# A Strassen-Winograd product schedule on one Trainium2 core: one block product moved two places forward, degree products spread between matmuls

## What is computed

```python
h   = xn @ gnn_W                                  # 1250x1024 by 1024x1024
deg = 1 + number of edges into a node;  dinv = deg ** -0.5
gnn = relu(segment_sum(h[src] * dinv[src] * dinv[dst], dst) + b)      # with self loops
mix = linear attention: relu(xn Wq + bq) (relu(xn Wk + bk)^T (xn Wv + bv)) Wo + bo
x   = x + gnn + mix
x   = x + ffn(layernorm(x))                       # 8-bit fake quantised gate, up and down
```

## Time and profile before

| what | us |
|---|---|
| median of three runs | 723.74 (723.11 to 725.48) |
| the profiled execution, time | 723.66 |
| its span in the trace | 721.9 |
| TensorE busy in the span | 703.2 |
| VectorE, GpSimd, ScalarE busy | 548.6, 347.2, 234.4 |
| block products of h (420 matmuls), first to last start | 362.2 to 457.1 |
| the ten degree products (20 passes) | 367.78 to 369.9 |

### The profile page before, as it was taken

How to read it: one execution, slowest core, us unless ns; L and a number is a source line. 1 busy time by engine, 2 the same in 40 slices (tenths; PEclk the granted TensorE clock), 3 DMA queues, 4 the chain that set the end, 5 groups by cost and what they waited for, 6 DMA issues and landing times.

```text
span 721.9 us, 11607 instructions
## 1 busy us (share of the span) xinstructions
PE 703.2 (97%) x3800; PEld 362.3 (50%) x3800; DVE 548.6 (76%) x1035; ACT 234.4 (32%) x384; POOL 347.2 (48%) x441
## 2 busy tenths in 40 slices
PE   5998999999999999999999999999999999999996
PEld 3454555545555554566654444444444444445752
DVE  7878887887666778876697865869977778766766
ACT  5133334553333356554223334530100000003641
POOL 3676767888666778874254540011111111113317
PEclk9999999999999999999999999999999999999999
DMA  9825413563000000000000005153322132100707
GB/s 347 253 59 118 109 36 83 169 238 120 0 0 0 1 2 1 1 0 1 1 1 0 1 1 177 56 175 67 100 73 57 50 84 65 35 12 1 118 1 284
DMA packets 52804, 52.27 MB, mean 72 GB/s; under 512 B 36515, under 2 KB 37547, under 8 KB 52753
## 3 DMA queue, kind: packets, MB, share of 16 engines
q1 hardware_dynamic: 52752, 51.61, 24.4%
HBM read 37.96 MB, written 5.12 MB: 60 GB/s over the span
## 4 chain that ended last, share of the span: by engine, by line
PE 77%; DVE 8%; issue 5%; POOL 3%; DMA 3%; SPq 2%; ACT 1%; DVEq 1%; POOLq 0%
PE bank L632 17%; PE bank L872 13%; PE bank L745 12%; PE bank L709 12%; PE bank L816 12%; PE bank L920 3%; PE bank L614 2%; DVE mem L1491 2%; PE bank L949 2%; DVE counts L1368 1%; PE bank L652 1%; PE bank L808 1%; DMA mem<-in_x 1%; POOL hot_src L490 1%; ACT mem L977 1%
## 5 line engine op out<-in xcount | busy, mean ns | idle before, releaser
L632 PE MATMUL bank<-mem 128*128 128x512 f16 x960 | 222.7, 381 | 0.0
L490 POOL TENSOR_SCALAR hot_src<-iota_p,src_col 125x128 bf16<-125x128 bf16 x252 | 189.6, 767 | 14.1 <-issue 14.1
L632 PEld LDWEIGHTS bank<-mem 128*128 128x128 f16 (+1 forms) x960 | 91.0, 98 | 95.6 <-issue 1.6
L1368 DVE TENSOR_TENSOR counts<-bank,counts 128x120 f32 x328 | 92.1, 281 | 43.3 <-PE bank L614 6.3
L872 PE MATMUL bank<-mem 128*128 128x512 f16 (+1 forms) x504 | 105.5, 369 | 0.0
L709 PE MATMUL bank<-mem 128*128 128x512 f16 (+2 forms) x576 | 105.1, 339 | 0.0
L745 PE MATMUL bank<-mem 128*128 128x512 f16 x420 | 92.8, 384 | 0.0
L816 PE MATMUL bank<-mem 128*128 128x512 f16 x400 | 88.0, 379 | 0.3 <-DVE mem L1674 0.3
L872 PEld LDWEIGHTS bank<-mem 128*128 128x128 f16 x504 | 49.3, 98 | 53.7 <-issue 0.3
L709 PEld LDWEIGHTS bank<-mem 128*128 128x128 f16 (+1 forms) x576 | 55.3, 98 | 41.3
L573 POOL TENSOR_TENSOR cols<-cols 128x1 f32<-128x1 f32 x10 | 5.5, 555 | 138.9 <-DVE cols L1701 138.9
(11 more groups left out here) (179 smaller groups left out, 828.9 us busy)
## 6 DMA issues: line engine op xcount, KB each, us to landing
mem<-in_x SPq DMA_DIRECT2D x18, 512.0 KB, 4.0
out_x<-mem SPq DMA_DIRECT2D x9, 512.0 KB
mem<-in_L_mix_Wk SPq DMA_DIRECT2D x4, 1024.0 KB, 9.6
mem<-in_L_mix_Wv SPq DMA_DIRECT2D x4, 1024.0 KB, 8.4
mem<-in_L_mix_Wq SPq DMA_DIRECT2D x4, 1024.0 KB, 5.1
mem<-in_L_gnn_W SPq DMA_DIRECT2D x4, 1024.0 KB, 7.5
mem<-in_L_mix_Wo SPq DMA_DIRECT2D x4, 1024.0 KB, 6.2
mem<-in_L_ffn_w_down SPq DMA_DIRECT2D x4, 352.0 KB, 3.2
```

The source lines that it names most:

```text
L490: pool.tensor_scalar(hot_src[0:EC, i, c, :], iota_p[0:EC, :], src_col[0:EC, i, c:c + 1], None, ALU.is_equal).then_inc(S["hot_src_ready"], 1)
L632: last = pe.matmul(o[:, :], xT[:, a * K + k, bass.ds(t * P, P)], w16[i][:, k, b, :], start=(at == 0), stop=(at == len(parts) - 1))
L1368: dve.tensor_tensor(window, agg[i][:, k * WC:(k + 1) * WC], window, ALU.add).then_inc(S["adj_added"], 1)
```

## The change

In all five pairs B21 becomes the third product: B11, T4, B21, T2, T1, T3, B22. The waits that count products in g_full are renumbered (T2 is now the fourth, T1 the fifth). b0 is thus finished in mid-pair, and for j > 0 its rounding (h_high and h_low of block 0) moves forward on ScalarE and VectorE. On ScalarE keep_p5(j) now comes behind s_high(j+1, 2). keep_p1(0) moves ahead of s_high(0, 4). In pair 0 the degree product of tile n is issued ahead of matmul n of T2, for the first ten of T2's twelve matmuls, and no longer as a block of its own ahead of T2.

```diff
@@ -383,7 +383,7 @@
             load_wo(0, 1)
             sp.wait_ge(S["g_full"], 7 * (PAIRS_OF_TILES - 1) + 1)
             load_wo(1, 0)
-            sp.wait_ge(S["g_full"], 7 * (PAIRS_OF_TILES - 1) + 4)
+            sp.wait_ge(S["g_full"], 7 * (PAIRS_OF_TILES - 1) + 5)
             load_wo(1, 1)
             sp.wait_ge(SM["prod_full"], PAIRS)
             sp.dma_start(gb_b, gnn_b.rearrange("(a n) -> a n", a=1).broadcast_to([P, D])).then_inc(SM["gb_in"], 16)
@@ -736,10 +736,19 @@
                                   stop=True).then_inc(SE["e_mm"], 1)
             q_blocks(2, 1)
 
-            def product(j, left, right, o, fresh):
+            def degree(n):
+                return pe.matmul(agg[0][:, n:n + 1], sources[:, n * P:(n + 1) * P], ones, start=True, stop=True,
+                                 skip_group_check=True)
+
+            def product(j, left, right, o, fresh, degrees=0):
 
                 for k in range(K // 2):
-                    for a, b in ((0, 0), (0, 1), (1, 0)):
+                    for pass_n, (a, b) in enumerate(((0, 0), (0, 1), (1, 0))):
+                        n = 3 * k + pass_n
+                        if n < degrees:
+                            counted = degree(n)
+                            if n == degrees - 1:
+                                counted.then_inc(SM["deg_full"], 1)
                         block = s_half[j % 2][:, 2 * (left - 1) + a, k, :] if isinstance(left, int) else \
                             block_at(left[1], 2 * j + left[0], a)[:, k, :]
                         last = pe.matmul(o[:, :], block, g_w[right][:, k, b, :], start=(fresh and k == 0 and a == b),
@@ -761,14 +770,10 @@
                     pe.wait_ge(S["h_lo"], 4 * (j - 2) + 2)
                 product(j, (1, 1), "T4", b2, True)
 
+                pe.wait_ge(SG["p1_kept"], j + 1)
+                product(j, (0, 1), "B21", b0, False)
                 if j == 0:
                     pe.wait_ge(SM["sources"], 1)
-                    for n in range(T):
-                        last = pe.matmul(agg[0][:, n:n + 1], sources[:, n * P:(n + 1) * P], ones, start=True, stop=True,
-                                         skip_group_check=True)
-                    last.then_inc(SM["deg_full"], 1)
-
-                if j == 0:
                     pe.wait_ge(S["q_lo"], 3 * K + 1)
                 elif j == 1:
                     pe.wait_ge(SM["deg_ready"], 1)
@@ -776,7 +781,7 @@
                 else:
                     pe.wait_ge(SG["u3"], j - 1)
                 pe.wait_ge(SG["s_lo"], 4 * j + 2)
-                product(j, 2, "T2", b1, True)
+                product(j, 2, "T2", b1, True, T if j == 0 else 0)
 
                 if j == 0:
                     pe.wait_ge(SM["max_col"], 1)
@@ -786,8 +791,6 @@
                     pe.wait_ge(S["h_lo"], 4 * (j - 2) + 4)
                 product(j, 1, "T1", b3, True)
 
-                pe.wait_ge(SG["p1_kept"], j + 1)
-                product(j, (0, 1), "B21", b0, False)
                 pe.wait_ge(SG["s_lo"], 4 * j + 4)
                 pe.wait_ge(SG["u2"], j + 1)
                 product(j, 3, "T3", b1, False)
@@ -1072,8 +1075,16 @@
                     act.wait_ge(S["g_full"], 7 * (j - 1))
                 act.activation(s_half[j % 2][:, 2 * (i - 1)], s_sum[i - 1], ACT.Copy).then_inc(SG["s_hi"], 1)
 
-            for i in range(1, 5):
+            def keep_p1(j):
+                act.wait_ge(S["g_full"], 7 * j + 1)
+                if j > 0:
+                    act.wait_ge(SG["u3"], j)
+                act.activation(g_s1, g_bank[j % 2][0][:, :], ACT.Copy).then_inc(SG["p1_kept"], 1)
+
+            for i in range(1, 4):
                 s_high(0, i)
+            keep_p1(0)
+            s_high(0, 4)
             act.wait_ge(SC["clip_in"], 32)
             act.activation(clip[:, 2:4], clip[:, 0:2], ACT.Exp, scale=-1.0).then_inc(SC["exp"], 1)
 
@@ -1083,14 +1094,14 @@
                                o.rearrange("p (k n) -> p k n", n=P), ACT.Copy, scale=dinv_up[:, t:t + 1]).then_inc(S["h_hi"], 1)
 
             def keep_p5(j):
-                act.wait_ge(S["g_full"], 7 * j + 4)
+                act.wait_ge(S["g_full"], 7 * j + 5)
                 if j > 0:
                     act.wait_ge(SG["c22"], j)
                 act.activation(g_s5, g_bank[j % 2][3][:, :], ACT.Copy).then_inc(SG["p5_kept"], 1)
 
             def wo_high(n, c):
                 act.wait_ge(SM[f"wo_in{n}_{c}"], 16)
-                act.wait_ge(S["g_full"], 7 * (PAIRS_OF_TILES - 1) + (7 if n else 3))
+                act.wait_ge(S["g_full"], 7 * (PAIRS_OF_TILES - 1) + (7 if n else 4))
                 act.activation(wo16[n][:, c * (K // 2):(c + 1) * (K // 2), 0, :], wo[n][c], ACT.Copy,
                                scale=W_UP).then_inc(SM["wo_hi"], 1)
 
@@ -1103,22 +1114,25 @@
             for j in range(PAIRS_OF_TILES):
                 last_pair = j == PAIRS_OF_TILES - 1
                 b0, b1, b2, b3 = g_bank[j % 2]
-                act.wait_ge(S["g_full"], 7 * j + 1)
                 if j > 0:
-                    act.wait_ge(SG["u3"], j)
-                act.activation(g_s1, b0[:, :], ACT.Copy).then_inc(SG["p1_kept"], 1)
+                    keep_p1(j)
                 if j + 1 < PAIRS_OF_TILES:
                     s_high(j + 1, 1)
+                if j > 0:
+                    act.wait_ge(S["g_full"], 7 * j + 3)
+                    h_high(2 * j, 0, b0[:, :])
+                if j + 1 < PAIRS_OF_TILES:
+                    s_high(j + 1, 2)
                     keep_p5(j)
-                    for i in range(2, 5):
-                        s_high(j + 1, i)
+                    s_high(j + 1, 3)
+                    s_high(j + 1, 4)
                 else:
                     wo_high(0, 0)
                     keep_p5(j)
                     wo_high(0, 1)
-                act.wait_ge(S["g_full"], 7 * j + 5)
-                act.wait_ge(SM["dinv"], 3)
-                h_high(2 * j, 0, b0[:, :])
+                if j == 0:
+                    act.wait_ge(SM["dinv"], 3)
+                    h_high(0, 0, b0[:, :])
                 act.wait_ge(SG["c21"], j + 1)
                 h_high(2 * j + 1, 0, b2[:, :])
                 act.wait_ge(SG["c22"], j + 1)
@@ -1511,7 +1525,7 @@
             dve.tensor_reduce(flags[:, 1:2], agg[1][0:1, 0:P], AX.X, ALU.max).then_inc(SM["max_col"], 1)
 
             def u2(j):
-                dve.wait_ge(S["g_full"], 7 * j + 3)
+                dve.wait_ge(S["g_full"], 7 * j + 4)
                 dve.wait_ge(SG["p1_kept"], j + 1)
                 if j > 0:
                     dve.wait_ge(SG["c12"], j)
@@ -1571,11 +1585,13 @@
             for j in range(PAIRS_OF_TILES):
                 b0, b1, b2, b3 = g_bank[j % 2]
                 more = j + 1 < PAIRS_OF_TILES
-                if j > 0:
-                    u2(j)
                 if more:
                     s_low(j + 1, 1)
                     s2(j + 1)
+                if j > 0:
+                    h_low(j, 1, 2 * j, 0, b0[:, :])
+                    u2(j)
+                if more:
                     s_low(j + 1, 2)
                     s_low(j + 1, 3)
                     s4(j + 1)
@@ -1585,7 +1601,8 @@
                     wo_low(0, 1)
                     dve.wait_ge(SM["wo_lo"], 2)
                     a_tile(0, 0)
-                h_low(j, 1, 2 * j, 0, b0[:, :])
+                if j == 0:
+                    h_low(0, 1, 0, 0, b0[:, :])
                 dve.wait_ge(S["g_full"], 7 * j + 6)
                 if j > 0:
                     dve.wait_ge(SG["c21"], j)
```

## The result

The changed kernel takes 729.12 us (median of four runs, 728.52 to 729.82), the kernel before 723.88 us: the ratio is 1.0074, 95% interval 1.0059 to 1.0089. The profiled execution took 728.52 us with a span of 726.7, against 723.66 and 721.9: 4.86 us more.

A forecast was written before the change was run, and what follows sets the result against it. TensorE, busy 703.2 of 721.9 us, was taken to bound the kernel. The later B22(0) (3.06), low clock (1.7) and last pair (2.0) summed to 6.8 us on 723.66, so 730.4 us, range 728.7 to 732.5.

The forecast's parts named there:

- the three terms of the sum: B22(0) starting 3.06 us later, 1.7 us of low clock after that stall, 2.0 us in the last pair.
- Degrees between T2's matmuls: Pair 0, T2: ten degree products at 0.22 us each cost 2.2 us, bounded by 1.05 and 3.4 us.
- B21 third in pair 0: Pair 0: keep_p1(0) in time, B21 covers the wait for `sources`, TensorE's stream taken alone gains 2.12 us.
- keep_p5(0) behind s_high(1, 2): Pair 0: B22(0) waits for VectorE's chain, a stall of 5.2 us, starting 3.06 us later than before.
- The clock after the stall: B22(0) and B11(1): they start at 1.2 GHz, one low stretch costing 1.7 us.
- Pairs 1 to 4: Earlier products of these pairs: nothing charged, keep_p1(1) ends 0.9 us before B21(1) is due.
- The last pair: Pair 4 and Wo: the fourth product of Wo comes 2.0 us later with TensorE idle, the clock staying up.
- a second one, as in the rival: Second low stretch after the last pair's wait or inside T2: 732.1 us, chance 0.19.
- The rival on the other side: Pair 0: keep_p5(0) is in time, only the stream's own 2.12 us gain is left: 721.5 us, chance 0.04.

The follow-up runs named there:

- twice: The pair 0 alone version with each degree product issued twice in its place: 726.60 us, ratio 1.0042 to the kernel before.
- degrees as a block: The pair 0 alone version with the ten degree products as one block again between B21 and T2: 721.36 us, ratio 0.9979 to the kernel before.
- wait filled: The changed kernel with 19 unused matmuls filling TensorE's wait ahead of B22(0): 729.82 us, ratio 1.0078 to the kernel before.
- pair 0 alone: The changed kernel with pairs 1 to 4 in the old order and keep_p5(0) ahead of s_high(1, 2): 721.30 us, ratio 0.9967 to the kernel before.
- three versions with the wait in three places: The changed kernel; it with keep_p5(0) ahead of s_high(1, 2); that plus u3(0), c21(0), keep_p1(1) earlier: 729.12, 728.69, 729.38 us.
- spreading alone: The kernel before with the degree products between T2's matmuls and B21 still fifth in every pair: 726.40 us, ratio 1.0047.

## Why the prediction was right, and where it was off

The sign, the range (728.7 to 732.5, measured 729.12) and the three terms of the sum were right in kind. The size was too large, 6.8 us against 4.9 in the profiled execution, mainly by two terms, and two readings beside the sum were wrong: why the clock had fallen before, and what would happen if keep_p5(0) were in time.

- *Degrees between T2's matmuls: mis-sized.* Taken at 0.22 us each, they cost 0.137, so T1 started at 373.99 in place of 374.89. The row I priced them from the earlier trace rows is a product with 128 columns, not one. It lay between the bounds of 0.11 and 0.34. Nor could that row speak against hidden loads, as I had it: two passes of 128 columns take some 0.11 us of the 0.22 for their columns alone, an estimate from the 0.053 us of a pass of 120 columns. By the Trainium skill, "TensorE: Matmul & The Clock Gate", section "Step-by-step: what each phase is for", the next weights load while the matmul before them runs. The trace agrees in part: a degree costs 0.09 us less of its 0.226 behind a long matmul, and in the "twice" run the second degree, behind a one-column pass, costs the full 0.22.
- *B21 third in pair 0.* keep_p1(0) ran at 364.94, B21 had no wait, as forecast. The stream's own gain is larger than the 2.12 us forecast: 2.96, shown by the version that keeps nothing but it; the cheaper degrees are the difference. Either figure contains the 1.7 us of the low stretch in the old T2.
- *keep_p5(0) behind s_high(1, 2): right, price too high.* The stall was 383.46 - 379.17 = 4.3 us, not 5.2. From the transpose to s_high(1, 2) it took 382.30 - 373.88 = 8.42 us where I carried over 9.14; 0.73 of that is the one tiny operation, L1523, that took 0.88 us before and 0.15 now; no row let me foresee it. B22(0) was 1.3 us later than before in place of 3.06. What I had not seen is that this wait covers the next: with the copy in its old place, the time does not improve.
- *The clock after the stall.* 1.7 forecast, 1.71 measured. That the clock falls with such a wait was right; that the block of degrees by itself had made it fall in the kernel before was wrong, as "degrees as a block" shows. My row for a clock that stays up over a shorter wait, 59 to 62 us, was luck of the execution: in the trace of "wait filled" the clock fell behind that same wait.
- *Pairs 1 to 4.* I charged nothing and gave keep_p1(1) 0.9 us to spare. It ended at 391.96, B21(1) started at 383.46 + 7.77 + 1.71 = 392.94. Right, but only since TensorE was late already.
- *The last pair.* 2.0 forecast, 1.9 measured; that the last pair's order makes it is shown by the run that takes it back. The clock stayed up in the trace, as taken. In two of the four executions the mean granted clock was 0.994, less than the one low stretch and the low clock after TensorE's last matmul can give, so a longer low stretch or a second one, as in the rival, must have come there; no trace shows which or where. The delay is the one worked out from the earlier trace rows.

The sum by the trace: 1.3 + 1.7 + 1.9 = 4.9 us. Against 6.8 the 0.8 us of the degrees and the 0.7 of the clip operation make most of the difference. The rival on the other side (keep_p5(0) in time, 721.5 us) was wrong in its "if, then": with keep_p5(0) in time the kernel takes 728.7 us. That pair 0 alone takes 721.3 us, near the rival's 721.5, is a coincidence: that kernel leaves pairs 1 to 4 in the old order, and its stream gains 2.96 us, not 2.12.

The cause of the loss is shown as far as the place and the length of TensorE's waits go. What stays open is which order of VectorE's queue, if any, would let B21 be third in pairs 1 and 2 without a wait; one other order was tried.

## What to carry to other kernels

A wait that appears on the bounding engine is not yet the cost of the line that placed it: put that line back alone and see whether the next wait takes its place; here three versions with the wait in three places had the same stretch within 0.35 us. When a reordering gains in one iteration only, because of something that only this iteration has to hide, apply it to that iteration alone. And price an added instruction by a row with its own shape and its own neighbours.

## What the runs showed of the hardware that was not expected

**The low clock comes and goes between executions of one kernel.** Each run gives the mean granted clock of the span. Of 45 timed executions of the kernel before beside the experiments, the nine with 1.000 took 721.49 to 722.92 us, the six with 0.993 or 0.994 took 724.66 to 725.18 us. So most of this kernel's spread (721.49 to 725.18 us, 0.5%) goes with how much of the execution was granted the low clock; which places lose it in the executions without a trace isn't known. The mean also counts some 1 to 3 us of low clock after TensorE's last matmul, which cost no time. The low stretch that the trace of the kernel before shows in T2 is therefore not part of every execution. Among executions with 0.998 or more, pair 0 alone has a median of 721.1 us (nine) and the kernel before beside it 722.0 us (three): by this estimate the larger part of its gain of 2.6 us is that the low clock comes less often.

**The same place kept the clock in one execution and lost it in another.** Early in the kernel, where no version differs, TensorE waits for about 2.2 us and goes on at 61.6 us. The first line is of the kernel before, the second of "wait filled":

```profile
62.00:65.00 3.00, 3.00 (x17) 1.24 (x15) 2.61 (x7) 0.80 (x2) 2.83 (x4) 1.00 0.55 104
```
```profile
62.32:65.76 3.44, 3.44 (x10) 1.22 (x8) 2.89 (x9) 0.45 (x2) 3.27 (x6) 0.50 0.58 109
```

The waits were 2.25 and 2.23 us long. So one trace doesn't show what a pattern of work does to the clock. As single traces are to be read: T2 with one degree per matmul kept its 2.4 GHz behind dense work (the changed kernel), lost it behind 2.2 us of idle time (spreading alone: 6.6 us low), and lost it with two degrees per matmul (6.9 us low). The block of 20 one-column passes kept it behind dense work, and lost it behind 0.4 us of idle time. The waits of 4.0 to 4.5 us lost it in each of the four traces that have one.

**A VectorE operation on 128x2 elements took up to six times its usual time beside GpSimd.** In the kernel before, and in the run with the degrees as a block:

```profile
375.43 0.88 DVE L1523 TENSOR_SCALAR clip<-clip 128x2 f32<-128x2 f32 x1
```
```profile
375.13 2.46 POOL L526 TENSOR_TENSOR mem<-mem 128x512 f32<-128x512 f32 x2
```
```profile
375.30 0.49 DVE L1549 TENSOR_SCALAR clip<-clip 128x2 f32<-128x2 f32 x1
```
```profile
374.60 2.46 POOL L527 TENSOR_TENSOR mem<-mem 128x512 f32<-128x512 f32 x2
```

The two GpSimd operations of the row take about 1.23 us each, so that the first ends at about 376.36 and 375.83. The VectorE operation started in its middle and ended at 376.31 and 375.79. In seven other traces it started 0.1 us ahead of the GpSimd operation and took 0.15 us. That it waits for the end of the other engine's operation is a reading of these times, not shown by an experiment: the one made for it hit the end of the operation. Nor does it hold for every GpSimd operation: in "degrees twice" it started at 378.32, inside GpSimd's operation on 128x10 elements (L552, from 376.93 for 1.99 us), and took 0.15 us. The Trainium skill, "GPSIMD Engine Reference", section "1. Specifications", says that GpSimd shares its SBUF interfaces with VectorE, with contention for VectorE instructions that have two SBUF inputs or run in a two-port mode. For the first kind the traces agree: s_low, s2 and s4, with two inputs in SBUF, took 1.3 to 1.6 us beside GpSimd's sums and 0.7 alone. Whether the operation on 128x2 elements, with one input, is of the second kind no trace here shows.
